# Language-model layer, first stage: query-key product ahead of the transposes, normed rows turned one step ahead, fewer small VectorE operations

## Chip, cores and metric

The kernel runs on one core of one Trainium2 chip. The time is the device time of one execution in microseconds (us). Lower is better.

## What is computed

The reference is one layer over 64 sequences of 128 token ids. Cut to what matters:

```python
h = concat(token_table[ids], category_table[ids])            # 64 x 128 rows of 256
# linear attention, 16 heads of 16
qkv = layernorm(h) @ W_qkv + b_qkv
pq, pk = elu(q) + 1, elu(k) + 1
kv = einsum('bshd,bshm->bhmd', pk, v)
z = 1 / (einsum('bshd,bhd->bsh', pq, pk.sum(1)) + 1e-6)
h = h + einsum('bshd,bhmd,bsh->bshm', pq, kv, z)
# experts: 16, the two best of each row
x2 = layernorm(h)
logits = l2norm(x2) @ l2norm(sim_matrix) - sigmoid(gates)
rw = softmax over the kept relu(logits)
q, k, v = (sum over experts of rw * (x2 @ proj[e]))
out = h + sum over experts of rw * (causal_softmax(q k^T) v @ o_proj[e])
```

## The kernel before

One tile is one sequence: 128 rows on the partitions, 256 columns. There are B = 64 tiles and three stages.

**First stage** (`step1` of every engine, run by `run1` for steps -7 to 67). In step i every engine works on several tiles, each at another point of the chain; `i.shift(k)` is tile i + k. GpSimd gathers the embedding rows of tile i + 7 (`gather_rows`, L623). VectorE forms the row statistics of tile i + 6 (`row_stats`, L970). The variances of one row of the table `moments` (L1107 for the first norm, L1127 for the second) get an epsilon (`roots_in`, L1133 and L1134), GpSimd raises them to the power -1/2 (`roots`, L688), and VectorE multiplies the means by the result (`centers`, L1070). Both norms of different tiles share one row: the first norm of tile r and the second norm of tile r - 3. ScalarE then writes the normed rows (`x1`, L815; `x2`, L822). TensorE transposes ("turns") `x1` into a PSUM bank (L1402), ScalarE rounds it to `split_hi` (L834), VectorE subtracts to get `split_lo` (L1103). TensorE makes the query-key product (512 columns, seven matmuls, L1417 and L1421) and the value product (256 columns, seven matmuls). ScalarE forms `qk_neg` and `qk_e` (L805, L809), VectorE `phi` (L1085). TensorE turns the query half of `phi` and makes the state product `kv` from the key half (L1476); VectorE masks it (`kvm`, L1118 and L1120); TensorE makes the attention sums (L1442); VectorE divides (`den` L1090, `zden` L1094, `attn` L1097) and adds (`h2`, L1112), then the statistics of the second norm (L1125). TensorE turns `x2` and makes the 16 router logits (L1453).

**Routing** runs in groups of four tiles (the last eight tiles in groups of two), one piece per step behind the group's last tile: `experts_chosen` (L994 to L1007), `experts_numbered` (L1016 to L1023), `rows_counted` (L1033 to L1042), `rows_placed` (L1050 to L1063). One step later GpSimd begins to scatter the group's `x2` rows to their places sorted by expert (L701): two indirect DMAs per tile, the second of which waits for `h2` of the same step; the tiles of the last five groups go two to a step, and their scatters do not wait for `h2`. VectorE also splits one expert weight matrix per step (L506, steps 8 to 55).

**Order.** Each engine executes its own `step1` strictly in the order in which it is written; semaphores (`after`, `done[...]`) are the only thing between engines. A wait therefore holds back everything that stands behind it on its engine. The order of TensorE in a step is: rank product (every fourth step), sums, logits, turn x1, turn phi, turn x2, state product, query-key product, value product. PSUM has one bank for the query-key product, one for `x1` turned, and so on; `x1T_s` (the two halves `split_hi`, `split_lo`) had one buffer.

Two rules of VectorE's order matter here:

```python
row = i.c + 4                      # at the head of the step
dve.wait_ge(done["roots"], row + 1)     # then centers
...
row = i.c + 5                      # behind the second norm's statistics
# roots_in of this row; GpSimd takes it at the head of its next step
```

**Second stage** (`step2`): the sorted rows are read back, multiplied by their expert's weights and stored. It begins once the last scatter has landed. **Third stage** (`step3`): causal attention and the output experts. Neither is touched by the change, except that GpSimd's address arithmetic between the stages first copies the positions from integers to floats.

## Time and profile before

| | |
|---|---|
| median of 3 runs | 1014.51 us (1014.26 to 1015.08) |
| the profiled execution's own time | 1013.34 us |
| span of its profile | 1011.6 us |
| TensorE busy | 928.0 us, 92% |
| VectorE busy | 836.3 us, 83% |
| ScalarE busy | 600.6 us, 59% |
| GpSimd busy | 632.1 us, 62% |
| first stage | from the start to about 388 us |
| chain that ended last | PE 55%, DVE 26%, POOL 8%, issue 6%, ACT 2%, DMA 2% |

PE is TensorE, DVE VectorE, ACT ScalarE, POOL GpSimd. A row of the timeline gives the start in us, the duration in us, engine, line, operation, output and input, and in brackets the idle time of the engine before it with what ended it. An instruction of VectorE or ScalarE can start while the one before it still drains, so what it costs its engine is the distance from its start to the start of the next one, which is often less than its duration.

### The profile page before, as it was taken

The numbers are of one execution on the slowest core, as the hardware profiler recorded it, in microseconds if no ns is written. First come the engines' busy times: TensorE is split into PE (matmuls) and PEld (weight loads), VectorE is DVE, ScalarE is ACT, GpSimd is POOL, SyncE is SP. The second block draws the span as 40 slices with busy tenths as digits, with TensorE's granted clock in tenths as the row PEclk, the third lists the DMA queues.
The fourth block names the chain that finished last, engine by engine and source line by source line (L and its number), as shares of the span: only waits on it lengthen the run. The fifth ranks groups of instructions, "written<-read, shape, count | busy, mean of one in ns | idle before, by whom it ended". The sixth has DMA issues, their size and how long they took to land.

```text
span 1011.6 us, 20470 instructions
## 1 busy us (share of the span) xinstructions
PE 928.0 (92%) x5230; PEld 800.2 (79%) x5230; DVE 836.3 (83%) x2884; ACT 600.6 (59%) x1633; POOL 632.1 (62%) x832
## 2 busy tenths in 40 slices
PE   4999999999999845999999959999999999999997
PEld 3787788788788734899999938888888888888876
DVE  4789999999999875655555539999999999999998
ACT  4666766666676511644444436666666666666664
POOL 5447777777777678100000058888888888888885
PEclk9999999999999956999999969999999999999999
DMA  2123344443333236898878633333333333333331
GB/s 65 48 74 120 121 142 150 143 146 126 122 125 117 93 109 215 264 298 260 258 248 265 227 116 104 103 104 103 104 104 105 101 105 106 103 105 104 91 105 37
DMA packets 106297, 137.53 MB, mean 136 GB/s; under 512 B 13762, under 2 KB 93634, under 8 KB 106180
## 3 DMA queue, kind: packets, MB, share of 16 engines
q1 hardware_dynamic: 87348, 83.98, 26.7%
q0 software_dynamic: 17408, 50.35, 16.4%
q10 hardware_dynamic: 1424, 1.84, 0.5%
q8 instruction: 49, 0.80, 0.3%
q14 instruction: 68, 0.56, 0.2%
HBM read 70.06 MB, written 66.06 MB: 135 GB/s over the span
## 4 chain that ended last, share of the span: by engine, by line
PE 55%; DVE 26%; POOL 8%; issue 6%; ACT 2%; DMA 2%; SPq 1%; POOLq 0%; DVEq 0%; ACTq 0%
PE bank L1395 15%; PE bank L1396 15%; PE bank L1397 15%; PE bank L1402 5%; DVE phi L1085 4%; DVE attn L1097 2%; DVE kvm L1118 2%; POOL sorted_x L701 2%; DVE stats L1125 2%; POOL row_y L776 2%; DVE stats L970 2%; DVE zden L1094 1%; PE bank L1421 1%; PE bank L1592 1%; PE bank L1598 1%
## 5 line engine op out<-in xcount | busy, mean ns | idle before, releaser
L1395 PE MATMUL bank<-wo_hi,split_lo 128*128 128x512 f32 x512 | 213.7, 417 | 1.5 <-DVE split_lo L1363 1.4
L1396 PE MATMUL bank<-wo_lo,split_hi 128*128 128x512 f32 x512 | 202.8, 396 | 0.0
L1397 PE MATMUL bank<-wo_hi,split_hi 128*128 128x512 f32 x512 | 202.2, 395 | 0.0
L776 POOL DMA_INDIRECT row_y<-sorted_y,pair_now x128 | 131.5, 1027 | 32.1 <-issue 22.9
L769 POOL COPY pair_now<-pair_at 128x2 uint32<-128x2 uint32 x64 | 12.2, 191 | 176.9 <-SPq L574 176.9
L900 ACT ACTIVATE h<-bank,rwo 128x256 f32<-128x256 f32 x256 | 107.2, 472 | 25.0 <-PE bank L1397 15.9
L1234 DVE TENSOR_TENSOR split_lo<-bank,split_hi 128x256 fp32r<-128x256 f32 x144 | 60.8, 422 | 68.6 <-ACT split_hi L861 67.1
L1397 PEld LDWEIGHTS bank<-wo_hi,split_hi 128*128 128x128 f32 x512 | 96.9, 189 | 22.5
L1395 PEld LDWEIGHTS bank<-wo_hi,split_lo 128*128 128x128 f32 x512 | 97.1, 190 | 20.6 <-DVE x L1332 1.6
L1332 DVE SCALAR_TENSOR_TENSOR x<-bank,rwo,x 128x256 f32<-128x256 f32 x256 | 111.1, 474 | 1.1 <-PE bank L1397 1.0
L1332 DVE SCALAR_TENSOR_TENSOR qk_e<-bank,rwo,qk_e 128x256 f32<-128x256 f32 x256 | 110.9, 474 | 0.3 <-PE bank L1397 0.2
L1396 PEld LDWEIGHTS bank<-wo_lo,split_hi 128*128 128x128 f32 x512 | 97.5, 190 | 16.9
L1395 PE MATMUL bank<-wq_hi,split_lo 128*128 x288 | 110.1, 382 | 0.0
L701 POOL DMA_INDIRECT sorted_x<-row_y,position_u x80 | 78.7, 984 | 44.0 <-DVE h L1112 29.7
L805 ACT ACTIVATE qk_neg<-bank 128x512 f32<-128x512 f32 x64 | 38.3, 599 | 112.4 <-PE bank L1421 112.4
L1397 PE MATMUL bank<-wq_hi,split_hi 128*128 x288 | 98.2, 341 | 0.0
L1396 PE MATMUL bank<-wq_lo,split_hi 128*128 x288 | 97.8, 340 | 0.0
L900 ACT ACTIVATE phi<-bank,rwo 128x256 f32<-128x256 f32 x128 | 53.8, 472 | 68.3 <-PE bank L1397 68.3
L1421 PE MATMUL bank<-wo_lo,split_hi 128*128 128x512 f32 (+1 forms) x256 | 87.3, 341 | 0.0
L861 ACT CAST split_hi<-bank 128x256 fp32r<-128x256 f32 x144 | 54.1, 375 | 55.7 <-PE bank L1402 55.4
L1421 PE MATMUL bank<-wo_hi,split_lo 128*128 128x512 f32 (+1 forms) x256 | 87.0, 340 | 0.0
L1421 PE MATMUL bank<-wo_hi,split_hi 128*128 128x512 f32 (+1 forms) x256 | 86.9, 339 | 0.0
(212 smaller groups left out, 2538.3 us busy)
## 6 DMA issues: line engine op xcount, KB each, us to landing
sorted_y<-row_y SPq DMA_DIRECT2D x36, 384.0 KB, 3.1
sorted_y<-w_attn SPq DMA_DIRECT2D x36, 384.0 KB, 3.2
row_x<-sorted_x SPq DMA_DIRECT2D x72, 128.0 KB, 2.9
h_rows<-h SPq DMA_DIRECT2D x64, 128.0 KB, 1.7
row_x<-h_rows SPq DMA_DIRECT2D x64, 128.0 KB, 3.5
out_h<-row_x SPq DMA_DIRECT2D x64, 128.0 KB, 2.1
phi<-sorted_x SPq DMA_DIRECT2D x36, 128.0 KB, 2.9
qk_neg<-sorted_x SPq DMA_DIRECT2D x36, 128.0 KB, 3.0
```

Of the source, the lines that this page charges most:

```text
L701: pool.indirect_dma_start(out=sorted_x, out_offset=offsets(position_u[:, t, n:n + 1]), in_=x2[t % N_X2], in_offset=None).then_inc(scattere ...
L776: pool.indirect_dma_start(out=row_y[:, 2 * tile.p + n, :], out_offset=None, in_=sorted_y, in_offset=offsets(pair_now[tile.q][:, n:n + 1])) ...
L861: act.copy(split[tile.q][0][:, :, :].rearrange("p c t -> p (c t)"), ps_turn[tile.p][:, 0:C]).then_inc(done["pair_hi"], 1)
L900: act.mul(part[:, j, :], ps[:, j * C:(j + 1) * C], rwo[tile.p][:, e:e + 1]).then_inc(o_scaled, 1)
L1085: dve.scalar_tensor_tensor(phi[:, :], ps_qk[:, :], 0.0, qk_e[:, :], ALU.max, ALU.add).then_inc(done["phi"], 1)
L1234: dve.tensor_tensor(lo, ps_turn[tile.p][:, 0:C], hi.bitcast(F32), ALU.subtract).then_inc(done["pair_lo"], 1)
L1332: dve.scalar_tensor_tensor(acc[j][:, :], src, weight, base[:, :], ALU.mult, ALU.add).then_inc(o_added, 1)
L1395: pe.matmul(ps, left[1][c], right[0][c], start=(c == 0), stop=False)
L1396: pe.matmul(ps, left[0][c], right[1][c], start=False, stop=False)
L1397: last = pe.matmul(ps, left[0][c], right[0][c], start=False, stop=(c == n - 1))
L1402: last = pe.transpose(ps[:, n * P:(n + 1) * P], piece, ident[:, :])
L1421: last = pe.matmul(ps[:, 0:hi - lo], turned[x][c], w_attn_s[w][:, c, lo:hi], start=False, stop=end)
```

## The change

On TensorE the query-key product stands right behind the logits, and the turn of `x1` is made for tile i + 5 instead of i + 4, behind the two other turns and ahead of the state product; `x1T_s` gets a second buffer for it. Everything that leads to `x1` moves a step earlier with it (gather of tile i + 8, statistics of tile i + 7, roots of row i + 5), and a row of `moments` now holds the second norm of tile r - 4. On ScalarE `v_copied`, `x1` and `x2` come first in the step; `qk_neg` and `qk_e` follow for tile i + 4 instead of i + 3. On VectorE: the mask of `kv` is one operation of 272 columns instead of two (TensorE's state product is 136 columns wide instead of 130); the third column of `roots_in` and its operation are gone; the row's energy for the router is now formed by two small operations at the head of the step (`energy_formed`) and a power on GpSimd (`energy`), new there; `is_one` and `is_two`, the two products `picked` and the two reductions are one operation each, and the copy to integers is gone. The pieces of VectorE's step are in another order.

```diff
-                for t in first_gathers.get(i.c, (i.c + 7,) if i.c >= -2 else ()):
+                for t in first_gathers.get(i.c, (i.c + 8,) if i.c >= -2 else ()):
                     gather_rows(Tile(t))
+                g = group_at(i.c)
+                if g is not None:
+                    n = GROUPS[g][1]
+                    quad_done(pool, "gate_scaled", g - 1)
+                    quad_done(pool, "energy_in", g)
+                    pool.tensor_tensor(energy[:, 0:n], energy_in[:, 0:n], minus_half[:, 0:n], ALU.pow
+                                       ).then_inc(done["energy"], 1)
...
-            first_gathers = {-5: (1,), -4: (2,), -3: (3, 4)}
+            first_gathers = {-6: (1,), -5: (2,), -4: (3,), -3: (4, 5)}
...
+            def energy_formed(g):
+                first, n = GROUPS[g]
+                rows = slice(first + 4, first + 4 + n)
+                quad_done(dve, "energy", g - 1)
+                dve.tensor_tensor(root_sq[:, 0:n], roots[:, rows, 1], roots[:, rows, 1], ALU.mult
+                                  ).then_inc(gate_own, gate_count("root_sq"))
+                gate_wait("root_sq")
+                dve.scalar_tensor_tensor(energy_in[:, 0:n], moments[:, rows, 1, 1], LN_EPS * NORM_EPS / C,
+                                         root_sq[:, 0:n], ALU.add, ALU.mult).then_inc(done["energy_in"], 1)
```

**VectorE, one step of the steady part** (the step of `rows_placed`). Before, from `centers` on:

```order
L1070 SCALAR_TENSOR_TENSOR centers<-moments,roots 128x2 [waits roots]
L506 TENSOR_TENSOR wq_lo<-raw,wq_hi 128x2x128 [waits weights_hi]
L1085 SCALAR_TENSOR_TENSOR phi<-bank,qk_e 128x512 [waits qk_exp,kv_product]
...
L1097 TENSOR_TENSOR attn<-bank,zden 128x256 [waits attn_z]
L1103 TENSOR_TENSOR split_lo<-bank,split_hi 128x256 [waits x1_T]
...
L1134 TENSOR_SCALAR roots_in<-moments 128x1
L1050 TENSOR_TENSOR ranks<-bank,region_start 128x64 [waits rank_product]
...
L1063 CAST position_u<-pair_in_x 128x8 [waits gate_own]
L970 BN_STATS stats<-h 128x6 [waits rows_gathered0]
```

and now:

```order
L1066 TENSOR_TENSOR picked<-is_pick,ranks 128x128 [waits ranks]
L1071 TENSOR_REDUCE position_u<-picked 128x2x4 [waits gate_own]
L1132 BN_AGGR moments<-stats 128x2 [waits ln2_stats]
L1138 TENSOR_SCALAR roots_in<-moments 128x2 [waits ln2_moments,ln1_moments]
L1144 TENSOR_TENSOR kvm<-bank,kv_mask 128x272 [waits kv_product,attn_sums]
L1149 TENSOR_TENSOR split_lo<-bank,split_hi 128x256 [waits x1_T]
L1079 SCALAR_TENSOR_TENSOR centers<-moments,roots 128x2 [waits roots]
L1001 TENSOR_TENSOR root_sq<-roots 128x4 [waits energy]
L1004 SCALAR_TENSOR_TENSOR energy_in<-moments,root_sq 128x4 [waits gate_own]
L506 TENSOR_TENSOR wq_lo<-raw,wq_hi 128x2x128 [waits weights_hi]
```

Before, a routing piece and the statistics of the next tile stood between `roots_in` and the wait of `centers`; now only the mask and `split_lo` do, and the routing piece stands ahead of `roots_in`.

**GpSimd, the step that ends a group of four.** Every step before the change has five rows like the last five of this fence; one step in four has the new second power:

```order
L688 TENSOR_TENSOR roots<-roots_in,minus_half 128x2 [waits roots_in]
L623 DMA h<-in_embed_table,ids 128x256
L701 TENSOR_TENSOR energy<-energy_in,minus_half 128x4 [waits energy_in,gate_scaled]
L708 DMA sorted_x<-x_6,position_u 135168x256 [waits position_index]
L708 DMA sorted_x<-x_6,position_u 135168x256 [waits h2]
```

The power of the energy stands between the gather and the scatters of that step.

**VectorE, the first operations of the program**, before:

```order
L970 BN_STATS stats<-h 128x6 [waits rows_gathered0,moments_set]
L1107 BN_AGGR moments<-stats 128x2 [waits ln1_stats]
L1133 TENSOR_SCALAR roots_in<-moments 128x2 [waits ln1_moments]
L1134 TENSOR_SCALAR roots_in<-moments 128x1
L946 TENSOR_TENSOR wo_lo<-w_attn,wo_hi 128x1536 [waits setup_a]
L1070 SCALAR_TENSOR_TENSOR centers<-moments,roots 128x2 [waits roots]
L952 TENSOR_TENSOR bias<-routing,bias 1x768 [waits setup_a]
```

and now:

```order
L979 BN_STATS stats<-h 128x6 [waits rows_gathered1]
L1138 TENSOR_SCALAR roots_in<-moments 128x2 [waits ln1_moments]
L1079 SCALAR_TENSOR_TENSOR centers<-moments,roots 128x2 [waits roots]
L1105 BN_AGGR moments<-stats 128x2 [waits ln1_stats]
L979 BN_STATS stats<-h 128x6 [waits rows_gathered2]
L1138 TENSOR_SCALAR roots_in<-moments 128x2 [waits ln1_moments]
L1149 TENSOR_TENSOR split_lo<-bank,split_hi 128x256 [waits x1_T]
L955 TENSOR_TENSOR wo_lo<-w_attn,wo_hi 128x1536 [waits setup_a]
L1079 SCALAR_TENSOR_TENSOR centers<-moments,roots 128x2 [waits roots]
L961 TENSOR_TENSOR bias<-routing,bias 1x768 [waits setup_a]
```

The waits for the second and third gather (`rows_gathered1`, `rows_gathered2`) now stand ahead of the split of the attention weights and of the bias, without which the first query-key product can't begin.

## Rows read from the trace of the kernel before

**Rows 1.** Timeline, VectorE: `phi` of step 8 and of step 55.

```profile
76.30 0.68 DVE L1085 SCALAR_TENSOR_TENSOR phi<-bank,qk_e 128x512 f32<-128x512 f32 x1
...
327.50 0.69 DVE L1085 SCALAR_TENSOR_TENSOR phi<-bank,qk_e 128x512 f32<-128x512 f32 x1
```

**Rows 2.** Timeline, VectorE, one step from `centers` on.

```profile
150.77 0.14 DVE L1070 SCALAR_TENSOR_TENSOR centers<-moments,roots 128x2 f32<-128x2 f32 x1
...
151.16 0.69 DVE L1085 SCALAR_TENSOR_TENSOR phi<-bank,qk_e 128x512 f32<-128x512 f32 x1
...
152.26 0.42 DVE L1097 TENSOR_TENSOR attn<-bank,zden 128x256 f32<-128x256 f32 x1
152.66 0.42 DVE L1103 TENSOR_TENSOR split_lo<-bank,split_hi 128x256 fp32r<-128x256 f32 x1
...
153.40 0.41 DVE L1118 TENSOR_TENSOR kvm<-bank,head_mask 128x256 f32<-128x256 f32 x1
...
153.81 0.41 DVE L1125 BATCH_NORM_STATS2 stats<-h 128x6 f32<-128x256 f32 x1
154.26 0.18 DVE L1127 BATCH_NORM_AGGREGATE moments<-stats 128x2 f32<-128x6 f32 x1
154.55 0.17 DVE L1133 TENSOR_SCALAR roots_in<-moments 128x2 f32<-128x2 f32 x1
...
154.69 0.21 DVE L1050 TENSOR_TENSOR ranks<-bank,region_start 128x64 f32<-128x64 f32 x1
...
155.67 0.42 DVE L970 BATCH_NORM_STATS2 stats<-row_x 128x6 f32<-128x256 f32 x1
```

**Rows 3.** Timeline, TensorE: turns, state product, first matmuls of the two products.

```profile
141.41 0.41 PE L1402 MATMUL bank<-ident,phi 128*128 128x128 f32 x2
...
141.90 0.63 PE L1476 MATMUL bank<-vx,phi 128*128 128x130 f32 x4
142.64 0.47 PE L1417 MATMUL bank<-bias,ones_r 128*128 128x512 f32 x1
...
144.34 0.28 PE L1417 MATMUL bank<-bias,ones_r 128*128 128x256 f32 x1
```

**Rows 4.** Timeline, GpSimd: the same step as Rows 2, and the power of 16 elements.

```profile
27.42 2.90 POOL L692 TENSOR_TENSOR sim_inv<-sim_norm,minus_half 128x16 f32<-128x16 f32 x1
...
150.63 1.03 POOL L623 DMA_INDIRECT row_x<-in_embed_table,ids  x1 [0.20 <-issue]
151.96 0.99 POOL L701 DMA_INDIRECT sorted_x<-row_y,position_u  x1 [0.30 <-issue]
153.76 0.97 POOL L701 DMA_INDIRECT sorted_x<-row_y,position_u  x1 [0.80 <-DVE h L1112]
154.86 0.88 POOL L688 TENSOR_TENSOR roots<-roots_in,minus_half 128x3 f32<-128x3 f32 x1
```

**Rows 5.** Timeline, VectorE: a step in which it waits for GpSimd's power.

```profile
27.46 0.19 DVE L1070 SCALAR_TENSOR_TENSOR centers<-moments,roots 128x2 f32<-128x2 f32 x1 [0.67 <-POOL roots L688]
```

**Rows 6.** Timeline, start of the program, GpSimd.

```profile
7.39 0.97 POOL L623 DMA_INDIRECT h<-in_embed_table,ids  x1 [0.28 <-POOL head_of_row L669]
8.40 1.99 POOL L688 TENSOR_TENSOR roots<-roots_in,minus_half 128x3 f32<-128x3 f32 x1
10.58 1.02 POOL L623 DMA_INDIRECT h<-in_embed_table,ids  x1 [0.19 <-issue]
```

**Rows 7.** Timeline, start of the program, VectorE.

```profile
12.46 0.42 DVE L1103 TENSOR_TENSOR split_lo<-bank,split_hi 128x256 fp32r<-128x256 f32 x1
...
13.40 0.43 DVE L970 BATCH_NORM_STATS2 stats<-h 128x6 f32<-128x256 f32 x1 [0.17 <-DMA h<-in_embed_table,ids]
...
17.63 0.69 DVE L1085 SCALAR_TENSOR_TENSOR phi<-bank,qk_e 128x512 f32<-128x512 f32 x1 [3.23 <-ACT qk_e L809]
```

**Rows 8.** Timeline, end of the first stage, GpSimd: power and scatter of step 59, scatter of step 63.

```profile
348.26 0.88 POOL L688 TENSOR_TENSOR roots<-roots_in,minus_half 128x3 f32<-128x3 f32 x1
349.46 1.03 POOL L701 DMA_INDIRECT sorted_x<-row_y,position_u  x1 [0.33 <-DVE position_u L1063]
...
368.66 1.02 POOL L701 DMA_INDIRECT sorted_x<-x,position_u  x1 [1.34 <-DVE position_u L1063]
```

More of the change, by code:

```diff
@@ L182, in build @@
         moments = sb("moments", [P, N_ROOTS, 2, 2])
-        roots_in = sb("roots_in", [P, N_ROOTS, 3])
-        roots = sb("roots", [P, N_ROOTS, 3])
+        roots_in = sb("roots_in", [P, N_ROOTS, 2])
+        roots = sb("roots", [P, N_ROOTS, 2])
         centers = sb("centers", [P, N_ROOTS, 2])
@@ L200, in build @@
         energy = sb("energy", [P, QUAD])
[L201 to L202 removed]
+        energy_in = sb("energy_in", [P, QUAD])
+        root_sq = sb("root_sq", [P, QUAD])
+        is_pick = sb("is_pick", [P, 2, QUAD, E])
         top_two = sb("top_two", [P, QUAD, E], F32R)
@@ L246, in build @@
                     for w in wo]
-        x1T_s = [w[:, :, :].rearrange("p c t -> p (c t)") for w in split[0]]
+        x1T_s = [[w[:, :, :].rearrange("p c t -> p (c t)") for w in split[n]] for n in range(2)]
         headsT = x1T[:, :].rearrange("p (a t) -> p a t", a=2)
@@ L802, in step1 @@
                 if tile.inside(B):
-                    after(act, "qk_product", tile)
-                    act.activation(qk_neg[:, :], ps_qk[:, :], ACT.Relu, scale=-1.0
-                                   ).then_inc(done["qk_negative"], 1)
-                    after(act, "qk_negative", tile)
-                    after(act, "phi", tile.shift(-1))
-                    act.activation(qk_e[:, :], qk_neg[:, :], ACT.Exp, scale=-1.0).then_inc(done["qk_exp"], 1)
-                tile = i.shift(4)
+                    after(act, "v_product", tile)
+                    after(act, "kv_product", tile.shift(-1))
+                    act.copy(vx[:, :, 0:P], ps_v[:, 0:C].rearrange("p (g n) -> p g n", g=G)
+                             ).then_inc(done["v_copied"], 1)
+                tile = i.shift(5)
                 if tile.inside(B):
@@ L820, in step1 @@
                     scatter_done(act, t - N_X2)
-                    after(act, "centers", tile.shift(3))
-                    act.activation(x2[t % N_X2], h2[tile.p][:, :], ACT.Identity, scale=roots[:, t + 3, 1:2],
-                                   bias=centers[:, t + 3, 1:2]).then_inc(done["x2_normed"], 1)
-                tile = i.shift(3)
-                if tile.inside(B):
-                    after(act, "v_product", tile)
-                    after(act, "kv_product", tile.shift(-1))
-                    act.copy(vx[:, :, 0:P], ps_v[:, 0:C].rearrange("p (g n) -> p g n", g=G)
-                             ).then_inc(done["v_copied"], 1)
+                    after(act, "centers", tile.shift(4))
+                    act.activation(x2[t % N_X2], h2[tile.p][:, :], ACT.Identity, scale=roots[:, t + 4, 1:2],
+                                   bias=centers[:, t + 4, 1:2]).then_inc(done["x2_normed"], 1)
                 tile = i.shift(4)
                 if tile.inside(B):
+                    after(act, "qk_product", tile)
+                    act.activation(qk_neg[:, :], ps_qk[:, :], ACT.Relu, scale=-1.0
+                                   ).then_inc(done["qk_negative"], 1)
+                    after(act, "qk_negative", tile)
+                    after(act, "phi", tile.shift(-1))
+                    act.activation(qk_e[:, :], qk_neg[:, :], ACT.Exp, scale=-1.0).then_inc(done["qk_exp"], 1)
+                tile = i.shift(5)
+                if tile.inside(B):
                     after(act, "x1_turned", tile)
-                    after(act, "v_product", tile.shift(-1))
-                    act.copy(x1T_s[0], ps_x1[:, 0:C]).then_inc(done["x1_T"], 1)
+                    after(act, "v_product", tile.shift(-2))
+                    act.copy(x1T_s[tile.p][0], ps_x1[:, 0:C]).then_inc(done["x1_T"], 1)
                 tile = i.shift(3)
@@ L990, in experts_chosen @@
                 tiles = slice(first, first + n)
[L991 removed]
                 ps = ps_logits[g % 2][:, 0:n, :]
                 after(dve, "logits_product", Tile(first + n - 1))
[L994 to L999 removed]
+                quad_done(dve, "energy", g)
                 dve.tensor_tensor(scaled[:, 0:n, :], ps, over_experts(energy[:, 0:n], n), ALU.mult
@@ L1417, in attn_product @@
                 pe.matmul(ps[:, 0:hi - lo], ones_r[:, :], bias[:, lo:hi], start=True, stop=False)
-                turned = [halves(x) for x in x1T_s]
+                turned = [halves(x) for x in x1T_s[tile.p]]
                 for c in range(CH):
@@ L1457, in step1 @@
                 if tile.inside(B):
-                    after(pe, "x1_lo", tile.shift(-1))
-                    after(pe, "x1_normed", tile)
-                    turn(ps_x1, *halves(x1)).then_inc(done["x1_turned"], 1)
+                    after(pe, "phi", tile.shift(-1))
+                    after(pe, "x1_lo", tile)
+                    if tile.c == 0:
+                        pe.wait_ge(setup_a, 4)
+                        pe.wait_ge(setup_v, 3)
+                    attn_product(tile, ps_qk, 0, 2 * C, "qk_product")
                 tile = i.shift(3)
@@ L1470, in step1 @@
                     turn(ps_x2, *halves(x2[tile.c % N_X2])).then_inc(done["x2_turned"], 1)
+                tile = i.shift(5)
+                if tile.inside(B):
+                    after(pe, "x1_lo", tile.shift(-1))
+                    after(pe, "x1_normed", tile)
+                    turn(ps_x1, *halves(x1)).then_inc(done["x1_turned"], 1)
                 tile = i.shift(3)
```

139 lines of the change are left out of this document (59 added, 80 removed).

## The prediction

> **What bounds the kernel now.** I began with the page's slices: the first stage has TensorE and VectorE both at nine tenths, so neither name alone says which one sets the step. The timeline of VectorE does. From step 8 to step 55 the step takes (327.50 - 76.30) / 47 = 5.345 us [rows 1], and in it VectorE goes from one operation to the next with hardly a wait [rows 2]. GpSimd's timeline has slack of one kind only: the second scatter waits 0.80 us for `h2` [rows 4]. The end of the stage is different: from step 59 on GpSimd issues scatters back to back (24 of them, and three powers), and VectorE waits for it [rows 8]; the last scatter's landing starts the second stage. So the stage has three parts: a start up to the first `phi`, some 60 steps, and a scatter tail. The later stages are untouched and I leave them at zero.
>
> **The step on VectorE.** Costs are distances between starts. From `centers` to `phi` is 0.39 us (0.06 and the weight split, 0.33), `phi` to `attn` 1.10, a 256-column pass 0.34, statistics to aggregate 0.45 when it has to wait for the result and 0.34 when it needn't, aggregate to `roots_in` 0.29 [rows 2]. The kernel before has 4.21 us of this per step without routing and without the wait of `attn` for `split_hi` (0.06), and routing takes the rest, 1.07 us per step.
> - One `kvm` pass for two: 0.41 becomes about 0.35 (272 columns for 256), -0.06. One `roots_in` for two: of the 0.14 us from `roots_in` to the routing piece [rows 2] some 0.06 goes.
> - The routing pieces: `rows_placed` is 0.98 us over six operations [rows 2]. It becomes three: 0.25 for the ranks, an estimated 0.31 for the wider product and 0.20 for the wider sum, 0.76. `is_pick` saves 0.07. The two energy operations (0.41) leave the piece and come back as 0.27 at the head of the step, where nothing waits behind the second. Routing falls from 1.07 to (4 x 1.07 - 0.22 - 0.07 - 0.41) / 4 = 0.89 us per step, plus 0.27 in one step of four.
> - The aggregate of the first norm hides in the wait of `zden` (-0.09) and the routing piece hides the wait of the second aggregate (-0.11), but `h2` is now followed at once by the statistics that need it (+0.12).
>
> VectorE alone would need about 4.00 + 0.89 + 0.07 = 4.96 us, against 5.28 and the waits: a gain of 0.38 per step if nothing else bound it. Two rings do.
>
> **Ring of TensorE.** From the start of `phi`: 0.69 its duration, 0.15 to the first matmul, 1.70 the query-key product (142.64 to 144.34), three turns at 0.25 (two take 0.49), 0.63 the state product, 0.03 to `kvm` [rows 3]: 3.95 us. Then 0.35 + 0.34 + 0.39 to the next `phi`: **5.03**. TensorE's own work is some 4.8 us, so it isn't the bound by itself. This is better than the old ring through `split_lo`, product, `qk_neg` and `qk_e`, which held `phi` back by up to 0.1 us in every other step.
>
> **Ring of the roots.** This is where I see the new wait. `roots_in` begins at `phi` + 1.10 + 0.35 + 0.34 + 0.43 + 0.34 + routing + 0.29 = 2.84 + routing. The power on GpSimd starts 0.25 us later (0.17 for the operation, 0.08 for the signal; 0.31 with two operations, 154.55 to 154.86 [rows 2, 4]). Its duration for two elements isn't in the trace. For three it is 0.88 us and for 16 it is 2.90 [rows 4], 0.155 us per element, so I take 0.72 for two and 1.03 for four; the bounds are 0.88 (no gain from one element less) and 0.59 (two thirds). `centers` follows its end by 0.04 [rows 5]. Before, a routing piece and statistics, 1.4 us, covered the power. Now `kvm` and `split_lo` do, 0.77 us, and the power takes 1.01 from the start of `roots_in`. So centers to centers is 0.39 + 2.84 + 1.01 = 4.24 + routing: 5.15 (numbered), 5.29 (counted), 5.00 (placed, where TensorE's ring of 5.03 binds).
>
> **GpSimd in the step of a group's end.** From power to power: 0.20, gather 1.03, 0.13, energy 1.03, 0.20, scatter 0.99, 0.30, scatter 0.97, 0.13, power 0.72 = **5.70** [rows 4]. VectorE's ring there is 5.36, so GpSimd sets this step. Four steps take 5.15 + 5.29 + 5.03 + 5.70 = 21.17 us against 21.38, a gain of 0.05 us a step. From step 8 to 55: **-2.4 us**.
>
> The Trainium skill (GPSIMD Engine Reference, section 3.1) gives about 2.6 cycles an element for a two-input operation on GpSimd behind a fixed dispatch: an element less would then save almost nothing. By it both powers keep 0.88, and the sum would be 5 us higher. Here the power of 16 elements took 2.90 us and that of three 0.88, so the trace disagrees for this operation, and I follow the trace.
>
> **The start.** The first `phi` is at 17.63, and the first product could begin when `split_lo` ended, 12.88 [rows 7]. Now the wait for gather 1 stands ahead of `roots_in`. Gather 1 is issued at 7.39 and a gather lands 2.82 us after its issue (10.58 to 13.40) [rows 6, 7]: 10.25. Then 0.35, 0.25, the first power of the program (1.99 less 0.16), 0.20, gather 2, 2.82: VectorE goes on at about 15.7. Then `roots_in` 0.35 and `split_lo` 0.42 later the weight split (1.7 us) and the bias (0.95) end at 19.3. From there the product and ScalarE take 17.63 - 12.88 = 4.75, and `split_lo` of tile 1, now ahead of `phi`, adds 0.75: first `phi` at about 24.8, **+7.2 us**. The bounds: +3 if gather 2 lands while the power runs, +9.
> Steps -3 to 8 have no scatters and no weight split, so TensorE's ring is 4.6 to 4.7 there against 5.3 before, with the routing steps dearer and GpSimd's 16-element power in one. Step by step I get 78.65 for `phi` of step 8 against 76.30: the eleven steps give back **-4.9**, and +2.3 remain.
>
> **The tail.** Steps 56 to 58 gain 0.5 us. At step 59 GpSimd's scatter came 0.32 us after the end of the power (348.26 + 0.88 to 349.46) [rows 8]; now the energy's power stands between: `centers`, two small operations and the signal 0.56, power 0.72, 0.20 = 1.5. So +1.0 with the shorter power, -0.2 at step 60, +1.1 at 61. At step 63 the scatter came 1.34 us after the last power [rows 8]; now the energy of the last group stands ahead of it, behind `rows_placed` and `experts_numbered`: 2.6, +1.2. Together **+3.2**, and nothing hides it, as GpSimd is the bound there. The copy of positions ahead of its address arithmetic is hidden behind the second stage.
>
> **Sum**: +2.3 - 2.4 - 0.5 + 3.2 = +2.6 us. Against the profiled execution's own 1013.34 that is 1016; the median is 1.2 us above it, so **1017**. A measurement of this kernel can tell about 0.2%, 2 us, from no change.
>
> **Rivals.**
> 1. VectorE and TensorE's rings hold alone (the powers on GpSimd are shorter than I think, or the waits are covered): four steps are 4 x 5.03 + 0.27 = 20.4 instead of 21.17, 9 us less: **1008**. For it: TensorE's queue is filled, and TensorE's ring of 5.03 is well read from rows. Against: it needs `roots` 0.3 us earlier in nearly every step. This ends faster. It decides from the point where a power of two elements takes under 0.5 us. Chance 0.2.
> 2. The start costs less (bound +3), the rest as forecast: 1013, no change. With a half of rival 1 it is the same. Chance 0.22.
> 3. The power is a fixed cost, 0.88 for two and for four: numbered and counted steps get 0.16, placed 0.13 dearer, the group's end stays; 0.45 per four steps, 5 us in the steady part and some 0.6 in the tail: **1022**. Against it stands the 16-element row. Chance 0.12.
> The forecast's own chance, with its sizes a little off, is 0.46.
>
> The range goes from 1009 to 1022. Slower by over 0.2% (above 1016.5): rival 3 and most of the forecast, 0.53. Faster (below 1012.5): rival 1 and a little of 2, 0.24. Same 0.23.
>
> **What would show it.** Right: `centers` waits for GpSimd's roots in three steps of four and the power of two elements takes 0.72; step 8's `phi` comes later than 76.30; the first `phi` near 24.8; step 59's scatter over a microsecond behind the power. Wrong: a step of 5.1 us or less in the steady part, with `kvm` waiting for TensorE's state product rather than `centers` for roots; or a first `phi` before 21.

## The result, and the profile after

The changed kernel takes 1020.25 us (median of 4 runs, 1019.59 to 1020.85), the kernel before 1014.80 us beside it (4 runs, 1014.26 to 1015.28). The ratio is 1.0052, with a 95% interval of 1.0040 to 1.0064: slower by half a per cent. The profiled execution took 1019.59 us, with a span of 1017.7 us and a granted clock of 0.971 (before 1013.34, 1011.6 and 0.973); 6.1 us of span have to be found.

The first part of the page is nearly that of before, and says as little:

```profile
PE 927.1 (91%) x5230; PEld 800.7 (79%) x5230; DVE 827.1 (81%) x2683; ACT 599.0 (59%) x1633; POOL 639.7 (63%) x852
```

VectorE is busy for 9 us less than before, as the change says, and the kernel is slower. The page's chain that ended last has shifted, though: VectorE fell from 26% of the span to 9%, and ScalarE rose from 2% to 6%, with `split_hi`, `pqT`, `x2T` and `wq_hi` at 1% each. ScalarE's queue now lies on the path. I went to the same places as ahead of the change. First `phi` on VectorE's timeline, as in [rows 1] and [rows 7]: the first one, that of step 8, that of step 55.

```profile
23.93 0.68 DVE L1096 SCALAR_TENSOR_TENSOR phi<-bank,qk_e 128x512 f32<-128x512 f32 x1
...
77.27 0.68 DVE L1096 SCALAR_TENSOR_TENSOR phi<-bank,qk_e 128x512 f32<-128x512 f32 x1
...
332.39 0.68 DVE L1096 SCALAR_TENSOR_TENSOR phi<-bank,qk_e 128x512 f32<-128x512 f32 x1
```

The first `phi` comes 6.30 us later than before, that of step 8 only 0.97 later, and that of step 55 again 4.89 later. The steady step is (332.39 - 77.27) / 47 = 5.428 us against 5.345. 46 of the 47 steps last 5.41 to 5.44 us, whether the routing piece and the two energy operations take 0.8 us in them or 1.2, and that is the first sign that neither VectorE's load nor the roots set it: both would give four different steps. (One step lasts 5.88: there GpSimd's second scatter began 1.00 us after the first ended instead of 0.30, and `centers` waited 0.82 us for the power. All the changed kernels but experiment 9 have one such step, and nothing here shows its cause.)

The waits of steps 8 to 55 (engine, line, releaser; us in all, times, longest):

```profile
ACT qk_neg L834 <- PE bank L1430: 84.0, 47, 1.8
...
POOL roots L688 <- DVE roots_in L1138: 20.1, 36, 0.7
...
DVE wq_lo L506 <- ACT wq_hi L501: 2.6, 15, 0.2
DVE centers L1079 <- POOL roots L688: 1.4, 2, 0.8
```

The list has two waits of VectorE for the roots, and 15 for `wq_hi`, the cast of a second-stage weight on ScalarE, of 0.17 us each. It can't be used for a count: it leaves out the small waits, and both of these are small. The rows show them. One step of GpSimd's and VectorE's timelines:

```profile
151.82 0.72 POOL L688 TENSOR_TENSOR roots<-roots_in,minus_half 128x2 f32<-128x2 f32 x1 [0.71 <-DVE roots_in L1138]
152.58 0.16 DVE L1079 SCALAR_TENSOR_TENSOR centers<-moments,roots 128x2 f32<-128x2 f32 x1
```

`centers` begins 0.04 us after the power has ended, and so it does (0.03 or 0.04) in every step from 8 to 55: it waits for the roots each time. But `wq_lo`, behind it, then waits again: it begins 0.45 or 0.46 us after the start of `wq_hi` in every step except the one of 5.88. So both waits are there, one behind the other, and the cast's ends last, 0.10 to 0.27 us after `wq_lo` could have begun. A ring is a chain of instructions, each of which needs the one before it, that comes back to its own start one step later; no step can be shorter than its ring. One step of the chain of waits (start, us, what) shows the one that binds:

```profile
158.53 0.69 DVE phi L1096
...
159.27 0.51 PE bank L1426
159.78 1.40 PE bank L1430 x6
161.17 0.66 PE bank L1411 x6
161.83 0.48 PE bank L1493 x4
...
162.37 0.35 ACT split_hi L843
162.73 0.27 ACT pqT L848
163.00 0.27 ACT x2T L854
163.27 0.31 ACT wq_hi L501
...
163.61 0.04 DVE wq_lo L506
...
163.95 0.69 DVE phi L1096
```

The ring is: `phi` lets TensorE make the query-key product; ScalarE turns it into `qk_neg` and `qk_e`, copies `split_hi`, `pqT` and `x2T`, and only then casts the weight; VectorE's `wq_lo` needs that cast and stands right ahead of the next `phi`. By starts, from ScalarE's and VectorE's timelines of the same step: `qk_neg` begins at `phi` + 2.68.

```profile
161.21 0.60 ACT L834 ACTIVATE qk_neg<-bank 128x512 f32<-128x512 f32 x1 [1.79 <-PE bank L1430]
161.84 0.63 ACT L838 ACTIVATE qk_e<-qk_neg 128x512 f32<-128x512 f32 x1
162.37 0.35 ACT L843 CAST split_hi<-bank 128x256 fp32r<-128x256 f32 x1
...
163.15 0.43 ACT L501 CAST wq_hi<-raw 128x256 fp32r<-128x256 f32 x1
...
163.61 0.43 DVE L506 TENSOR_TENSOR wq_lo<-raw,wq_hi 128x256 fp32r<-128x256 f32 x1 [0.15 <-ACT wq_hi L501]
```

2.68 + 0.63 + 0.53 + 0.78 + 0.46 + 0.34 = 5.42 us.

In the kernel before, the cast stood ahead of the `qk_neg` that the next `phi` needs, since that `qk_neg` came at the head of ScalarE's next step (155.14 us). `wq_lo` began 3.01 us after its cast, and waited for nothing:

```profile
153.05 0.43 ACT L501 CAST wq_hi<-raw 128x256 fp32r<-128x256 f32 x1
...
156.06 0.42 DVE L506 TENSOR_TENSOR wq_lo<-raw,wq_hi 128x256 fp32r<-128x256 f32 x1
```

GpSimd, the step with the energy. [rows 4] is the ordinary step of before, which has four instructions and not five: a power, a gather and two scatters.

```profile
156.97 0.71 POOL L688 TENSOR_TENSOR roots<-roots_in,minus_half 128x2 f32<-128x2 f32 x1 [0.43 <-DVE roots_in L1138]
157.88 1.03 POOL L623 DMA_INDIRECT row_x<-in_embed_table,ids  x1 [0.20 <-issue]
158.94 1.04 POOL L701 TENSOR_TENSOR energy<-energy_in,minus_half 128x4 f32<-128x4 f32 x1
160.19 1.03 POOL L708 DMA_INDIRECT sorted_x<-x,position_u  x1 [0.20 <-issue]
161.52 0.97 POOL L708 DMA_INDIRECT sorted_x<-x,position_u  x1 [0.30 <-issue]
162.55 0.71 POOL L688 TENSOR_TENSOR roots<-roots_in,minus_half 128x2 f32<-128x2 f32 x1
```

The power takes 0.71 for two elements and 1.04 for four, power to power is 5.58. VectorE's `centers` came 5.59 after the one before it (157.71 to 163.30), and `phi` was not late: at 163.30 `centers` still had 0.23 us to spare before the cast let `wq_lo` go.

The start, on VectorE, as in [rows 7]:

```profile
10.52 0.43 DVE L979 BATCH_NORM_STATS2 stats<-h 128x6 f32<-128x256 f32 x1 [3.09 <-DMA h<-in_embed_table,ids]
...
14.93 0.43 DVE L979 BATCH_NORM_STATS2 stats<-h 128x6 f32<-128x256 f32 x1 [2.82 <-DMA h<-in_embed_table,ids]
...
15.67 1.75 DVE L955 TENSOR_TENSOR wo_lo<-w_attn,wo_hi 128x1536 fp32r<-128x1536 f32 x1
```

VectorE stands idle for 5.9 us, for two gathers, ahead of the split of the attention weights, which ends at 17.4. The end, on GpSimd, as in [rows 8]; the last row is the last scatter, which before began at 382.72 us:

```profile
352.16 0.72 POOL L688 TENSOR_TENSOR roots<-roots_in,minus_half 128x2 f32<-128x2 f32 x1 [1.01 <-DVE roots_in L1138]
353.49 0.69 POOL L701 TENSOR_TENSOR energy<-energy_in,minus_half 128x2 f32<-128x2 f32 x1 [0.61 <-DVE energy_in L1004]
354.36 1.04 POOL L708 DMA_INDIRECT sorted_x<-row_y,position_u  x1 [0.18 <-issue]
...
389.68 0.96 POOL L708 DMA_INDIRECT sorted_x<-row_y,position_u  x1 [0.30 <-issue]
```

Where the 6.1 us of span are: +0.97 up to step 8; +3.92 from step 8 to 55; -0.39 from there to the last `phi` (360.06 us, before 355.56); +2.46 from the last `phi` to the last scatter (29.62 us, before 27.16), so that the last scatter is 6.96 us late; -2.08 from there on, nearly all of it because its landing took 2.58 us instead of 4.56, so that the second stage's first matmul comes at 395.84 instead of 390.96; and +1.2 over the 620 us of the later stages.

The shorter landing goes with the late scatter. The second stage waits for more than the last scatter (`regions_filled`, L540): sixteen transfers of zeros, of 128 KB each, fill the ends of the experts' regions (L459), eight from ScalarE's queue and eight from SyncE's. SyncE's eight, before and after:

```profile
377.29 6.10 SPq L459 DMA_DIRECT2D sorted_x<-zeros  x8
```

```profile
381.91 5.15 SPq L459 DMA_DIRECT2D sorted_x<-zeros  x8
```

They begin 21.73 us behind the last `phi` before and 21.85 after, and the DMA engines are full beside them (a share of 0.96 to 1.04 from 378 to 386 us before, 1.02 to 1.03 from 384 to 390 after). Before, the last scatter was issued 5.43 us behind the first of these fills, after the change 7.77, and it landed faster by 1.98. From the last `phi` to its landing it is 31.72 us before and 32.20 after: of the +2.46 only +0.48 is left.

### The profile page after: what moved, and what is told of

Read it like the earlier page. It is cut to its first block, busy times and chain, and to the rows that moved or that the text cites. A ratio compares the mean times of both kernels' runs of the same rounds, so it can differ in the third digit from the quotient of the medians.

```text
span 1017.7 us, 20322 instructions
## 1 busy us (share of the span) xinstructions
PE 927.1 (91%) x5230; PEld 800.7 (79%) x5230; DVE 827.1 (81%) x2683; ACT 599.0 (59%) x1633; POOL 639.7 (63%) x852
## 4 chain that ended last, share of the span: by engine, by line
PE 72%; DVE 9%; ACT 6%; issue 5%; POOL 5%; DMA 2%; POOLq 0%; ACTq 0%; SPq 0%; DVEq 0%
PE bank L1404 17%; PE bank L1405 16%; PE bank L1406 16%; PE bank L1411 8%; PE bank L1430 7%; DVE phi L1096 4%; PE bank L1426 2%; PE bank L1493 2%; POOL sorted_x L708 2%; ACT split_hi L843 1%; PE bank L1601 1%; PE bank L1607 1%; ACT wq_hi L501 1%; ACT pqT L848 1%; ACT x2T L854 1%
```

## The experiments

Each was run with the kernel before beside it on the same chip; where no other is named, a time stands against that kernel's 1014.2 to 1015.0 us. All compute the whole reference.

**1. The cast ahead of `qk_neg`.** One move on ScalarE in the changed kernel:

```diff
+                for n in weights_at(i.c):
+                    weight_hi(act, n)
                 tile = i.shift(4)
                 if tile.inside(B):
                     after(act, "qk_product", tile)
...
-                for n in weights_at(i.c):
-                    weight_hi(act, n)
```

> The changed kernel with one move: ScalarE casts the weight matrix of the step (wq_hi) ahead of qk_neg, in the 1.8 us in which it waits for the product anyway. Theory (weight ring): in the changed kernel phi, product, qk_neg, qk_e, split_hi, pqT, x2T, wq_hi, wq_lo, phi is a closed ring of 5.42 us and sets every step from 8 to 55. Without it the roots ring and GpSimd's long step bind, on average 5.29 us, so 48 steps give back about 6 us: 1014 us against 1020.25. Rival (the forecast's roots ring and GpSimd already set the step, the wait for wq_hi of 0.15 us is only where the slack happens to lie): no change, 1020.

Measured: 1015.42 us (10 runs, 1014.01 to 1017.50), ratio to before 1.0008 (0.9998 to 1.0018), not to be told from no change. The steady step fell to (326.87 - 77.19) / 47 = 5.312 us, and `wq_lo` begins 3.9 us or more behind its cast. Steps 8 to 55 became 5.4 us shorter, the median 4.8. The rival (no change) falls. What binds now is the ring that was forecast, as VectorE's timeline of this kernel shows:

```profile
155.82 0.16 DVE L1078 SCALAR_TENSOR_TENSOR centers<-moments,roots 128x2 f32<-128x2 f32 x1
...
160.14 0.17 DVE L1137 TENSOR_SCALAR roots_in<-moments 128x2 f32<-128x2 f32 x1
161.64 0.16 DVE L1078 SCALAR_TENSOR_TENSOR centers<-moments,roots 128x2 f32<-128x2 f32 x1 [0.48 <-POOL roots L688]
```

In three steps of four `centers` stands 1.01 us behind `roots_in`; the two rows above are the fourth, that of the energy, where GpSimd is late by 0.5. From `centers` to `centers` the four steps (at 150.81, 155.82, 161.64, 166.79 and 172.08 us) are 5.01, 5.82, 5.15 and 5.29 us; the forecast had 5.03, 5.70, 5.15 and 5.29. In the step of 5.01 the two forecast rings lie together: `kvm` begins 3.87 us behind `phi` (155.09 against 151.22; the forecast had 3.95), directly behind TensorE's state product, as in three steps of four, and `centers` again 0.04 us behind the power.

**2. The start reordered.** On VectorE of the changed kernel the splits of the weights and of the bias and the statistics change places in the first steps:

```diff
-                if i.c == -4:
+                if i.c == -5:
                     bias_split()
...
-                if stats_tile.inside(B):
+                if stats_tile.inside(B) and i.c not in (-6, -5, -4):
                     row_stats(stats_tile, 1 - i.p)
...
-                if i.c == -5:
+                if i.c == -6:
                     attn_weights_split()
+                if stats_tile.inside(B) and i.c in (-6, -5, -4):
+                    row_stats(stats_tile, 1 - i.p)
```

> The changed kernel with the start of VectorE's program reordered: in the first three steps the row statistics, which wait for a gather, come last, and the split of the attention weights and of the bias come ahead of them. Theory (start): the first phi comes at about 18.6 us instead of 23.9, and nothing behind it takes that back, since the steps from there on are ring-bound: 5 us less, 1015. Rival (the later gathers or the slow clock hold the second and third phi, and the steps up to 8 give the gain back): 1 us or less, 1019 or more.

Measured: 1015.21 us (10 runs, 1014.61 to 1016.80), ratio 1.0011 (1.0001 to 1.0021). The weight split begins at 8.17 us instead of 15.67, the first `phi` at 19.05 instead of 23.93, and these 4.9 us are kept: step 8 at 72.35, step 55 at 327.48, the last scatter at 384.77, each 4.9 us earlier, with the same step of 5.428. The theory holds, and the rival (the steps up to 8 give it back) falls.

**3. Energies back on VectorE.** The powers have three columns again, with two `roots_in` operations, and GpSimd has no energy:

```diff
-                    dve.tensor_scalar(roots_in[:, row, :], moments[:, row, :, 1], LN_EPS, None, ALU.add
-                                      ).then_inc(done["roots_in"], 1)
+                    dve.tensor_scalar(roots_in[:, row, 0:2], moments[:, row, :, 1], LN_EPS, None, ALU.add)
+                    dve.tensor_scalar(roots_in[:, row, 2:3], moments[:, row, 1, 1:2], LN_EPS * NORM_EPS / C, None,
+                                      ALU.add).then_inc(done["roots_in"], 1)
```

> The changed kernel with the row energies back on VectorE (third column of roots, two small products in the routing piece) and no second power on GpSimd. Theory (tail): from step 57 on GpSimd is the bound, and its three energy powers with their waits cost 3.2 us there; the steady steps stay at 5.42 us because the weight ring sets them. So 3 us less, 1017. Rival (GpSimd's long step of 5.70 us sets the pace of the steady part): another 12 x 0.3 us less, 1013. Third outcome: the three-column power (0.88 us) and the longer routing piece make the steady step 5.5 us and cost 4 us: 1021.

Measured: 1024.70 us (4 runs, 1023.78 to 1026.29), ratio 1.0098 (1.0081 to 1.0115): slower than any expectation. The tail did nearly what the theory said: the last `phi` to the last scatter is 27.02 us instead of 29.62, 2.6 us back where 3.2 was expected, but the landing took 4.20 instead of 2.58. The theory's steady part failed, and the third outcome named the reason with too small a size. The step is 5.532 us, and the list of waits of this kernel now has the forecast's line, in nearly every step:

```profile
DVE centers L1067 <- POOL roots L688: 12.9, 45, 0.7
```

From `roots_in` to `centers` it is 1.22 us instead of 1.01 (0.06 for the second operation, 0.16 for the third column's power), in every step, and the energy's 0.41 us lie in the ring where `experts_chosen` stands ahead of `roots_in`. So moving the energy to GpSimd and dropping a column was no loss in the steady part but worth 0.1 us a step; the theory had taken it that the cast's ring leaves room for it, and the roots' ring had only 0.10 to 0.27 us of room.

**4. Only the merged operations, in the kernel before.** One `kvm` pass, one `is_pick`, one product and one reduction in `rows_placed`; the order of all engines as before:

```diff
-                    dve.tensor_tensor(kvm[:, :, 0:P], ps_kv[:, :, 0:P],
-                                      head_mask[:, :].unsqueeze(1).broadcast_to([P, G, P]), ALU.mult)
...
+                    dve.tensor_tensor(kvm[:, :, :], ps_kv,
+                                      kv_mask[:, :].unsqueeze(1).broadcast_to([P, G, NUMW]), ALU.mult
+                                      ).then_inc(done["kv_masked"], 1)
```

> The kernel before with only the merged VectorE operations: one mask pass of kv, one comparison for both picks, one product and one reduction straight to integers; order, depth and energies as before. Theory (two rings lie together in the old kernel): VectorE's own work falls by 0.13 us per step, but the ring split_lo, product, qk_neg, qk_e, phi of 5.27 us then holds the step, so at most 0.07 us per step is won: 1012 to 1014 against 1014.8. Rival (VectorE alone bounds the old kernel): 0.13 us in some 56 steps, 7 us less: 1007.

Measured: 1013.47 us (10 runs, 1011.66 to 1015.89), ratio 0.9990 (0.9980 to 1.0001), not to be told from no change and inside the theory's 1012 to 1014; the rival (1007) falls. The step went from 5.345 to 5.323 us although VectorE has some 0.15 us less to do: in the old order `phi` then waits for `qk_e` (12 times, 3.3 us in all), and half of the steps stand at 5.28. One of these waits, in VectorE's timeline of this kernel:

```profile
155.84 0.69 DVE L1080 SCALAR_TENSOR_TENSOR phi<-bank,qk_e 128x512 f32<-128x512 f32 x1 [0.28 <-ACT qk_e L809]
```

**5. The routing piece behind `roots_in`**, together with the cast of experiment 1:

```diff
-                for back, piece in ((3, rows_placed), (2, rows_counted), (1, experts_numbered), (0, experts_chosen)):
...
                 row = i.c + 6
                 if 0 <= row < N_ROOTS:
...
+                for back, piece in ((3, rows_placed), (2, rows_counted), (1, experts_numbered), (0, experts_chosen)):
+                    g = group_at(i.c - back)
+                    if g is not None:
+                        piece(g)
                 if phi_tile.inside(B):
```

> ScalarE casts the weight before it takes qk_neg, as in the first experiment, and VectorE's routing piece stands behind roots_in instead of ahead of it. Theory (two rings, one behind the other: the cast first, the roots second): in the first experiment centers came exactly 1.01 us behind roots_in, and the routing piece stood in that ring (5.15, 5.28, 5.28, 5.55 us). With the routing behind roots_in, 0.57 us of slack covers the power, the ring of TensorE (5.03) binds, and the steady step is 5.05 to 5.18: 1003 to 1009 us. Rival A (the first experiment's step is VectorE's own load and no ring): moving the piece changes nothing, step 5.31, 1015. Rival B (GpSimd's load binds once the rings are loose, power to power 5.58 in one step of four, not recovered): step 5.18, 1009; then GpSimd's roots are late in that step alone.

Measured: 1007.05 us (4 runs, 1006.78 to 1008.18), ratio 0.9920 (0.9900 to 0.9940). The step is 5.175 us and its four values are 5.31, 5.25, 5.04 and 5.02. `centers` begins 0.05 us or more behind the end of the power in all steps but the long one: the routing covers the power. Rival A (nothing changes) falls. The time lies in the theory's range, and rival B's step of 5.18 is met too, but the mechanism of neither holds in full. TensorE's ring, which the theory has binding, is seen in one step of four, that of `rows_placed` (`kvm` 3.87 us behind `phi`, directly behind the state product). GpSimd's roots, which rival B has late, are not. In the other steps VectorE goes from one operation to the next without a wait that the rows show, and their sum is its own load. That load is larger than in the order before this edit: the routing piece no longer hides the distance from the second norm's statistics to their aggregate, which is now 0.46 us in every step (155.88 to 156.34 us), where a pass that isn't held takes 0.34.

**6. The energy one step earlier**, in the changed kernel, on VectorE and GpSimd:

```diff
-                g = group_at(i.c)
+                g = group_at(i.c + 1)
                 if g is not None:
                     energy_formed(g)
```

> The changed kernel with the energy of a group formed and raised one step earlier on VectorE and GpSimd, so that it no longer stands between the power of the roots and the scatters of steps 59, 61 and 63. Theory (the tail's loss is the energy's power in the way of the scatters, about 1.2 us each): it gives back 1.5 to 2.5 us of the 7 that the last scatter came later, 1018. Rival (the last scatter is late because the last steps of VectorE are late, not GpSimd): within 0.5 us of the changed kernel, 1020.

Measured: 1022.67 us (4 runs, 1020.16 to 1023.58), ratio 1.0067 (1.0043 to 1.0091). Neither expectation of the time holds. The tail did what the theory says: from the last `phi` to the last scatter 28.01 us instead of 29.62, 1.6 us back, though the landing took 0.8 us more (3.38 instead of 2.58). But the steady step rose to 5.484. The energy's step is now the one of `rows_placed`, and GpSimd's 5.8 us from power to power no longer lie beside the longest ring of VectorE but beside the shortest:

```profile
160.33 0.16 DVE L1079 SCALAR_TENSOR_TENSOR centers<-moments,roots 128x2 f32<-128x2 f32 x1 [0.49 <-POOL roots L688]
```

That step takes 5.56 us, and the others take 5.42 or more as before: 2.6 us more from step 8 to 55, and 1.5 more ahead of step 8. The gain in the tail was given back more than twice, since I had looked at the tail alone.

**7. All four edits**, that is the diffs of experiments 1, 2, 5 and 6 in the changed kernel:

> The changed kernel with four edits: the cast of the weight ahead of qk_neg, VectorE's start reordered (weight and bias split before the waits for the gathers), the routing piece behind roots_in, the energy one step earlier. Theory (the losses are separate and add up): the cast and routing give 1020 - 1006 = 14, the start 5, the tail 2: 997 to 1002. Rival (the steady gain is lost at the end, because GpSimd's queue of gathers and scatters sets a floor for the stage of about 60 x 5.0 us plus tail): not below 1006.

Measured: 1000.82 us (4 runs, 999.64 to 1002.23), ratio 0.9864 (0.9842 to 0.9887): 14 us faster than the kernel before, 19 faster than the change as it was made, and inside the theory's 997 to 1002. The rival (not below 1006) falls. The step is 5.170 us (5.59, 4.98, 4.97, 5.03), and of VectorE's waits between 77 and 315 us this one is left, and one of 0.2 us:

```profile
DVE centers L1078 <- POOL roots L688: 0.8, 1, 0.8
...
```

**8. The cast added to experiment 3**, that is the diffs of experiments 1 and 3.

> The third experiment (energies on VectorE, powers of three columns) with the weight cast ahead of qk_neg too. Theory (in the third experiment the ring of the roots bound 45 steps of 47, longer by 0.21 us with 1.22 instead of 1.01 from roots_in to centers, so the cast no longer matters): 1023 to 1024.5, the third experiment's time. Rival (the cast's ring still binds some of its steps, as it bound all steps of the changed kernel): the cast brings what it brought before, 5 us, 1019.5.

Measured: 1020.98 us (4 runs, 1020.47 to 1021.80), ratio 1.0061 (1.0040 to 1.0082): 3.7 us less than experiment 3. The theory (the cast no longer matters) falls. The rival had the mechanism, the cast's ring in some of the steps, but not the size (3.7 us instead of 5). The steps are 5.468 instead of 5.532 although VectorE waits for the roots in 46 of them. In experiment 3 `wq_lo` begins 0.46 us behind the start of `wq_hi` in every second step, the distance at which it waited for the cast in the changed kernel; in experiment 8 it never does. From `centers` to `phi` all rings share one stretch. In four steps of experiment 3, from the `centers` at 149.92 us to that at 166.65, `wq_lo` began 0.13, 0.08, 0.27 and 0.08 us behind `centers`, and in those of experiment 8 always 0.07 or 0.08, the distance that needs no wait. The excess of 0.25 us in four steps is the 0.064 us a step by which the two kernels differ: a small wait for the cast lay inside the ring of the roots and lengthened it.

**9. TensorE's queue put back**, in experiment 7: turns and state product first, the query-key product behind them.

```diff
-                tile = i.shift(4)
-                if tile.inside(B):
-                    after(pe, "phi", tile.shift(-1))
-                    after(pe, "x1_lo", tile)
...
-                    attn_product(tile, ps_qk, 0, 2 * C, "qk_product")
...
+                    attn_product(tile, ps_qk, 0, 2 * C, "qk_product")
                 tile = i.shift(4)
                 if tile.inside(B):
                     after(pe, "v_copied", tile.shift(-1))
```

> The seventh experiment (all four edits) with TensorE's queue alone put back: turn of x1, turn of phi, turn of x2, state product, and only then the query-key product; the rows are still turned a step ahead and ScalarE's order stays. Theory (the product stands first because it feeds ScalarE's qk_neg and qk_e, behind which its normed rows wait): a ring closes over ScalarE and TensorE: exp to the end of x2 2.6 us, turn 0.25, state product 0.63, product and signal 1.84, qk_neg 0.63, together about 5.95 us a step instead of 5.14, over some 60 steps 48 us: 1040 to 1050. Rival (in the seventh experiment VectorE's own work is the bound, and kvm and split_lo come 0.6 us later than TensorE's state product allows, so that TensorE's order no longer matters): 1001 to 1005.

Measured: 1061.20 us (4 runs, 1059.86 to 1062.75), ratio 1.0460 (1.0440 to 1.0481). The step is 6.057 us. The rival falls, and the time is 11 us above the theory's range. The ring isn't quite the one that it names; it closes over `pqT` and the attention's product, not over the turn of `x2`, as the chain of waits of this kernel shows:

```profile
152.29 0.61 ACT qk_neg L836
...
153.81 0.28 ACT pqT L850
...
154.34 0.70 PE bank L1453 x4
155.04 0.35 PE bank L1464 x4
155.39 0.78 PE bank L1413 x6
156.17 0.48 PE bank L1487 x4
156.65 0.24 PE bank L1428
156.89 1.41 PE bank L1432 x6
158.32 0.61 ACT qk_neg L836
```

**10. Experiment 7 without the early energy**, that is the diffs of experiments 1, 2 and 5.

> The seventh experiment without the early energy: cast, start and routing. Theory (start and steady part are separate; the early energy is worth 1.6 us in the tail, the last phi to the last scatter being 29.62 us without it and 28.0 with it, and nothing in the steady part, where VectorE's load of 20.56 us in four steps binds with and without it): 1002.0 to 1002.8. Rival (with the routing moved, the early energy costs in the steady part as it did in the sixth experiment, 0.06 us a step): 998 to 1000, faster than the seventh.

Measured: 1002.86 us (4 runs, 1002.51 to 1003.16), ratio 0.9888 (0.9872 to 0.9905). The step is 5.169 us against 5.170: with the routing moved, the early energy costs nothing in the steady part. From the last `phi` to the last scatter it is 29.57 us against 27.99, the 1.6 us of the theory. But the theory had left out three other places where the two kernels differ. The `phi` of step 8 comes at 72.70 us without the early energy and at 71.60 with it, from step 55 to the last `phi` it is 27.85 us against 25.85, and the landing takes 2.60 against 3.37. Together the second stage's first matmul is 4.0 us earlier with the early energy (375.26 against 379.24), the profiled span 2.8 us shorter, and the median 2.0.

## Why the prediction was right, and where it was not

The forecast was 1017.0 us, a range of 1009 to 1022 and 0.53 for slower. The kernel is slower, at 1020.25, in the range. But that both came true is in good part luck. The steady part, which was to gain, lost, and it is that loss which makes the kernel measurably slower: without it (experiment 1) what the prediction did foresee gives a kernel that can't be told from the one before (ratio 1.0008, 0.9998 to 1.0018). By its steps, against the profiled execution:

- **The powers.** Forecast 0.72 us for two elements and 1.03 for four, from [rows 4]; measured 0.71 to 0.73 and 1.04, and 0.69 for the energy of two. The rival with a fixed cost per power falls. The Trainium skill (GPSIMD Engine Reference, section 3.1) has about 2.6 cycles an element for a two-input operation, behind a fixed dispatch. For this operation the trace disagrees: one element of a row less was worth 0.16 us.
- **The start.** Forecast +7.2 us, measured +6.30. The reason holds, and experiment 2 gave 4.9 of it back. Mis-sized was "the first power of the program (1.99 less 0.16)": it took 0.73. (The sum also has slips: 7.39 + 2.82 is 10.21 and not 10.25, and 15.7 + 0.35 + 0.42 + 1.7 + 0.95 is 19.1 and not 19.3.) The steps up to 8 gave back 5.33 us where -4.9 was forecast, so +0.97 remained instead of +2.3.
- **The steady step.** Forecast -2.4 us, measured +3.92: **this is the step that failed.** The prediction said "Two rings do", TensorE's and the roots', and both were right: experiment 1 shows them at 5.01, 5.82, 5.15 and 5.29, and with them steps 8 to 55 are 1.5 us shorter than before (249.68 us against 251.20). There was a third, tighter one of 5.42 us, through the cast. Before and after, `phi` needs the `qk_neg` and `qk_e` of its own tile. Before, ScalarE made them at the head of its next step, behind the cast; now it makes them in the same step ahead of the cast, so that the cast comes late. I had costed the query-key product moved ahead as a gain on TensorE, and "from `centers` to `phi` is 0.39 us" with `wq_lo` in it as pure duration, without asking who releases `wq_lo`. The cast itself was not moved by the change; what it waits behind was.
- **What would show it.** `centers` was to wait for the roots in three steps of four. It does so in every step, 0.03 or 0.04 us behind the power, and still the roots don't set the step, since `wq_lo` behind it waits longer. The sign came true and didn't tell the right mechanism from the wrong one; a step of the same length in all four kinds would have. VectorE's own load was forecast at 4.96 us; what experiments 5, 7 and 10 show as its load, 5.17, is that of another order (see experiment 5).
- **GpSimd's step of 5.70.** Measured 5.58 from power to power in the changed kernel, where the cast's ring hid it, and 5.8 in experiment 1, where the first scatter took 1.28 us instead of 1.03.
- **The tail.** Forecast -0.5 and +3.2 (its terms add up to 3.1), together +2.7; measured +2.07 (-0.39 and +2.46). At step 59 power to scatter is now 354.36 - 352.88 = 1.48 us, as forecast. Experiment 6 gave 1.6 us of it back. What failed here is "nothing hides it, as GpSimd is the bound there": the landing took 1.98 us of the 2.46 back. It goes with the distance to the fills of zeros, for which the second stage also waits and which came only 0.12 us later behind the last `phi`; that they are the cause is argued and not shown.
- **Left out**: the end of the scatters to the second stage (-2.08) and the later stages (+1.2).

So +2.6 was forecast and +6.1 measured in the span: the steady part was missed by 6.3 us, and the other terms together by 2.8 the other way. For experiment 1, the kernel with the forecast's rings, 1017.0 would have been 1.6 us too high. Rival 1, "VectorE and TensorE's rings hold alone: 1008", comes near experiment 5 (1007.05 us), where the waits for the power are covered by the routing and not by a shorter power; its four steps are 20.7 us there against the rival's 20.4. Whether VectorE could go below the load of experiment 7 wasn't tried.

## What to carry to other kernels

When a product is moved ahead so that the next step's critical work depends on it, list what stands behind it in the queue of the engine that takes the result: each small copy or cast there enters the ring if anything ahead of the critical operation needs it. A step that stayed at 5.42 us whatever varying work it held was bound by a ring here, while rings through the varying work gave four different steps; follow the chain once round and add up starts. Don't count waits from a list that leaves out small ones: an engine can wait twice in a step, and only the wait that ends last sets it. Where an engine computes something short for another, put the other's independent work between the request and its use (here the routing piece between `roots_in` and `centers`: 8 us). While the request still lies open, put two long pieces on different engines into the same step, not into neighbouring ones (experiment 6); once it was covered, this no longer mattered in the steady part (experiments 7 and 10). And ask of a tail what else the next stage waits for: here the last scatter was issued 2.46 us later behind the last `phi` and landed 0.48 later.

## What the runs showed of the hardware

- A power on GpSimd took 0.69 to 0.73 us for 2 elements a row, 0.88 for 3, 1.04 for 4 and 2.90 for 16 [rows 4]: 0.155 us per element and some 0.4 us beside.
- The first power of the program ended at 10.36 to 10.62 us in the six kernels where it was asked for at once, behind the first gather (before, experiments 2, 4, 7, 9 and 10), and so took 1.73 to 1.99 us from its start at 8.40 to 8.77. Asked for at 11.0 to 11.2 it took 0.73 for two elements (after, experiments 1, 5 and 6) and 0.89 for three (experiments 3 and 8). What holds it until 10.4 isn't shown.
- The landing of the last scatter goes with its distance behind SyncE's first fill of zeros, in all twelve kernels: 5.43 us behind it, 4.56 us (before); 6.04 to 6.08 behind, 4.20 to 4.28 (experiments 3, 4 and 8); 6.50 to 6.53 behind, 3.37 to 3.43 (experiments 6, 7 and 9); 7.76 to 7.78 behind, 2.55 to 2.63 (after, experiments 1, 2, 5 and 10). The second stage's first read began 11.2 to 11.7 us behind that fill in all of them. That the full DMA engines cause it is argued from the shares beside the fills; no run moves or removes them.
